# Three score banks and single vector steps in the head loop of a recurrence stage, with its maxima and constants moved into the first stage

## The reference

```python
q = layernorm(x); k = v = ctx
ig, fg = [q, k, v] @ Wi + bi, [q, k, v] @ Wf + bf            # (b, 16, 512)
log_D = tril(cumsum(log_sigmoid(fg)) differences) + ig       # (b, 16, 512, 512)
D = exp(log_D - max(log_D))
C = (qh @ kh.T / sqrt(32)) * D
h = (C / (max(|C.sum|, exp(-max)) + 1e-6)) @ vh
h = (h - mean) * rsqrt(var + 1e-6) * ln_scale                # over the 32 columns of a head
x = x + tanh(g) * h
```

## Time and profile before

| what | us |
| --- | --- |
| median of three runs | 1750.79 |
| profiled execution, its own time | 1748.16 |
| its span | 1746.40 |
| recurrence stage within it | 0 to 369.25 |
| first multiplication of a head (L645) starts | 94.29 |
| last head's product is added to OUT (L628) | 344.15 |
| PE, DVE, ACT, POOL busy in the span | 1389.4, 1243.4, 767.4, 321.9 |

### The profile page before, as it was taken

How to read it: one execution, slowest core, us unless ns; L and a number is a source line. 1 busy time by engine, 2 the same in 40 slices (tenths; PEclk the granted TensorE clock), 3 DMA queues, 4 the chain that set the end, 5 groups by cost and what they waited for, 6 DMA issues and landing times. The chain is left out here.

```text
span 1746.4 us, 24792 instructions
## 1 busy us (share of the span) xinstructions
PE 1389.4 (80%) x9060; PEld 788.7 (45%) x9060; DVE 1243.4 (71%) x1952; ACT 767.4 (44%) x1450; POOL 321.9 (18%) x233
## 2 busy tenths in 40 slices
PE   3589899735568798987487696877999999999997
PEld 2367677521233344433354464533444444444443
DVE  4354666676256777895799999858778877788764
ACT  2433444335334354432688797823333333333322
POOL 0021142244555455754000000000000000000000
PEclk9777888755789899999798798989999999999998
DMA  7012133214533324222503000000000000000000
GB/s 254 3 51 71 61 121 97 73 53 149 146 101 98 117 89 129 85 98 101 200 2 120 24 0 0 0 1 4 9 6 6 6 12 6 6 6 6 12 6 12
DMA packets 56494, 102.19 MB, mean 59 GB/s; under 512 B 9823, under 2 KB 20727, under 8 KB 56300
## 3 DMA queue, kind: packets, MB, share of 16 engines
q1 hardware_dynamic: 55148, 97.14, 17.1%
q0 software_dynamic: 1280, 4.20, 0.9%
HBM read 73.47 MB, written 27.66 MB: 58 GB/s over the span
## 5 line engine op out<-in xcount | busy, mean ns | idle before, releaser
L2047 PE MATMUL HG<-W1H,XT 128*128 128x512 f16 x512 | 166.7, 388 | 27.2 <-ACT XT L2008 20.7
L1521 PE MATMUL FD<-W0D,HH 128*128 128x512 f16 x512 | 159.2, 394 | 14.6 <-DMA W0D<-down_weights,IDX 11.0
L2047 PE MATMUL HU<-W1H,XT 128*128 128x512 f16 x512 | 163.2, 380 | 0.0
L2073 PE MATMUL HD<-W1H,HT 128*128 128x512 f16 x512 | 155.3, 380 | 0.0
L1515 PE MATMUL FG<-F,W0G 97*128 97x512 f16 x324 | 84.4, 394 | 49.8 <-DMA F<-features_kept 23.3
L318 ACT ACTIVATE DD<-E,TM 128x128 f32<-128x128 f32 x256 | 72.6, 370 | 115.8 <-PE E L411 115.6
L1768 ACT ACTIVATE PR<-A_S,NM,CM 128x512 f32<-128x512 f32 x128 | 99.5, 777 | 34.4 <-DVE NM L1909 34.4
L2016 ACT ACTIVATE SG<-HG,DS 128x512 f32<-128x512 f32 x64 | 43.9, 686 | 160.3 <-PE HU L2047 160.3
L2150 DVE SCALAR_TENSOR_TENSOR H<-HU,DS,SG 128x512 f32<-128x512 f32 x64 | 48.0, 750 | 87.4 <-ACT SG L2016 85.4
L1405 POOL TENSOR_TENSOR HL<-HM,HH 128x512 f16<-128x512 f32 x64 | 92.5, 1445 | 82.6 <-ACT HH L1444 82.0
L1521 PE MATMUL FD<-W0D,HL 128*128 128x512 f16 x256 | 100.8, 394 | 0.0
(11 more groups left out here) (333 smaller groups left out, 3376.7 us busy)
## 6 DMA issues: line engine op xcount, KB each, us to landing
VALP<-in_ffn_weights_dram SPq DMA_DIRECT2D x24, 512.0 KB, 3.5
VALQ<-in_ffn_weights_dram SPq DMA_DIRECT2D x24, 512.0 KB, 3.6
quantised_weights<-QQ SPq DMA_DIRECT2D x24, 512.0 KB, 2.8
X<-in_x_dram SPq DMA_DIRECT2D x8, 1024.0 KB, 6.2
CTX<-in_ctx_dram SPq DMA_DIRECT2D x8, 1024.0 KB, 5.5
W1H<-quantised_weights SPq DMA_DIRECT2D x3, 2048.0 KB, 10.5
W1L<-quantised_weights SPq DMA_DIRECT2D x3, 2048.0 KB, 15.2
F<-features_kept SPq DMA_DIRECT2D x16, 288.0 KB
```

Of the source, the lines that this page charges most:

```text
L1521: last = pe.matmul(DN[c][:, :], lhs[:, i, c * P:(c + 1) * P], W2[:, i, part, :], start=(i == 0 and n == 0), stop=(i == KI - 1 and n == 2))
L2047: ins = pe.matmul(bank[:, :], lhs, rhs, start=(i == 0), stop=(i == len(terms) - 1))
L2073: ins = pe.matmul(DN[0][:, :], HT[:, q, lp, k, :], W[:, 2, i * D:(i + 1) * D], start=(i == 0 and lp == 0 and W is WH), stop=(i == KI - 1 a ...
```

## The change

PSUM bank T[1] becomes a third score bank: head n uses QK[n % 3]; read_state writes T[0] too, and state(n) waits for take_read(n - 1). `scores` waits for one head less. DVE goes head by head, with one optional step behind each; where the steps stand is given by lists. Eleven of the 24 maxima stand in the first stage, and their loads on SP before the stores of the NP parts. The fillers behind weigh(2 pair) and behind scores are left out. The first scores and two decays stand ahead of the first state, and ACT takes the first state behind head 1. The block in front is gone: X of batch 0 is the first load, the constants are made between batch 0 and batch 1, WG and GLN are loaded behind batch 1's context, and ACT does the deviation of batch 1 before batch 0's copies, that of batch b + 1 before batch b's copies. MV and SD have a place for each batch.

```diff
+FINISH_HEADS = (2, 12)
+COEF_HEADS = (0, 1, 13, 14, 15)
+PEAKS_FIRST = 11
+PEAK_HEADS = {2: (0, 1, 4, 8, 13, 14, 15), 3: (1, 4, 8, 13, 14, 15)}
...
-    T = [ps("T0"), ps("T1")]
-    QK = [ps("QK0"), ps("QK1")]
+    T = [ps("T0")]
+    QK = [ps("QK0"), ps("QK1"), ps("QK2")]
...
             for b in range(B):
-                if b:
-                    sp.dma_start(X[:, b * NC:(b + 1) * NC, :], xr[b]).then_inc(x_in[b], 16)
+                sp.dma_start(X[:, b * NC:(b + 1) * NC, :], xr[b]).then_inc(x_in[b], 16)
+                if b == 0:
+                    sp.dma_start(CST[:, :], A["shape_constants"]).then_inc(consts_in, 16)
+                    for q, name in enumerate(("g_xattn", "g_ffn")):
...
                 sp.dma_start(ctx_room[b], ctx[b]).then_inc(ctx_in[b], 16)
-                if b == 0:
+                if b == 1:
...
             spline.load(sp)
+            peaks.transfers(sp, 0, PEAKS_FIRST)
...
                     sp.dma_start(CTX[:, :, :], ctx[b + 1]).then_inc(ctx_again, 16)
-                peaks.transfers(sp, b)
                 if b == 0:
+                    peaks.transfers(sp, PEAKS_FIRST, PEAKS_FIRST + 2)
+                elif b == 1:
                     spline.store(sp)
+                else:
+                    done = PEAKS_FIRST + 2 + sum(len(PEAK_HEADS[i]) for i in range(2, b))
+                    peaks.transfers(sp, done, min(Q_TILES, done + len(PEAK_HEADS[b])))
...
-            act.wait_ge(pre_dve, PRE_DVE)
+            act.wait_ge(eps_ready, 3)
+            deviation(0)
+            act.wait_ge(consts_in, 3 * 16)
+            nc.scalar.activation(tg[:, :], tg[:, :], ACT.Tanh).then_inc(tanh_ready, 1)
             act.wait_ge(pre_pool, 3)
+            deviation(1)
             for b in range(B):
-                deviation(b)
+                if b >= 1 and b + 1 < B:
+                    deviation(b + 1)
...
                 if pair:
-                    pe.wait_ge(c_ready, 2 * pair)
+                    pe.wait_ge(c_ready, 2 * pair - 1)
...
                 if n:
-                    pe.wait_ge(state_taken, n)
+                    pe.wait_ge(read_taken, n)
...
+            pe.wait_ge(tm_taken, 2)
+            scores(0)
+            decay(0)
+            decay(1)
+            pe.wait_ge(tm_taken, 5)
             state(0)
-            scores(0)
-            for n in range(4):
-                decay(n)
+            decay(2)
+            decay(3)
             for pair in range(HEADS // 2):
                 ahead = 2 * pair + 4
                 weigh(2 * pair)
-                fill(ahead)
                 decay(ahead)
                 if pair % 2 == 0:
                     read_state(pair // 2)
                     fill(ahead + 1)
                 if pair + 1 < HEADS // 2:
                     scores(pair + 1)
-                    fill(ahead + 1)
                 weigh(2 * pair + 1)
...
+            for n in range(PEAKS_FIRST - 2):
+                peaks.peak(v, n)
...
             own(v.tensor_scalar(MZ, ZF, 0.0, None, ALU.min))
             owned()
+            peaks.peak(v, PEAKS_FIRST - 2)
...
             v.tensor_tensor(RR, NM, PARTS3[:, 0:S], ALU.subtract).then_inc(r_ready, 1)
+            peaks.peak(v, PEAKS_FIRST - 1)
...
+            for n in range(HEADS):
+                b, h = divmod(n, NH)
...
+                if h % HG == 1:
+                    take_read(n // HG)
+                if n % 2 == 0 and n:
+                    take_pair(n // 2 - 1)
+                if b == 0 or (b == 1 and h in COEF_HEADS):
                     next(coefficients, None)
+                if b and FINISH_HEADS[0] <= h <= FINISH_HEADS[1]:
+                    if h == FINISH_HEADS[0]:
                         v.wait_ge(o_taken, b * PAIRS)
+                    next(last_batch, None)
+                if b >= 2 and h in PEAK_HEADS[b]:
+                    peaks.peak(v, peak)
+                    peak += 1
```

More of the change, by code:

```diff
@@ L320, in _ @@
                     ins.then_inc(d_ready, 1)
-                    if n % HG == HG - 1 and n > HG and n // HG < HEADS // HG:
+                    if n == 1:
+                        take_state(0)
+                    elif n % HG == HG - 1 and n > HG:
                         take_state(n // HG)
@@ L356, in gates @@
                 pe.wait_ge(t_taken, 16 * pair + 16)
+                if pair == 0:
+                    pe.wait_ge(pre_dve, PRE_DVE)
                 for k in range(2 * KD):
@@ L484, in pre, with constants, gate_weights @@
                 ins.then_inc(pre_dve, 1)
[L486 to L496, removed]
+            v.memset(EPS[:, 0:1], 1e-5).then_inc(eps_ready, 1)
+            v.memset(EPS[:, 1:2], 1.0).then_inc(eps_ready, 1)
+            v.memset(EPS[:, 2:3], 1e-6).then_inc(eps_ready, 1)
+            def constants():
+                pre(v.memset(ONE[:, :], 1.0))
+                v.wait_ge(consts_in, 3 * 16)
+                pre(v.tensor_copy(idb, idf))
+                pre(v.tensor_copy(idh, idf))
+                for c in range(NC):
+                    pre(v.tensor_copy(FUT[:, c, :], CST[:, P:2 * P]))
+                pre(v.tensor_copy(PICK[:, :], CST[:, 2 * P:2 * P + NH]))
+            def gate_weights():
+                v.wait_ge(w_loaded, 3 * 16)
+                pre(v.tensor_tensor(WG[:, 4:8, :], WG[:, 4:8, :], WG[:, 8:12, :], ALU.add))
+                v.wait_ge(tanh_ready, 1)
+                pre(v.tensor_scalar(GLN[:, :], GLN[:, :], tg[:, 0:1], -1.0, ALU.mult, ALU.mult))
+                assert n_pre[0] == PRE_DVE
             n_own = [0]
@@ L517, in _ @@
                 v.wait_ge(sd_ready, b + 1)
-                own(v.reciprocal(RS[:, :], SD[:, :]))
+                own(v.reciprocal(RS[:, :], SD[:, b, :]))
                 owned()
@@ L635, in _ @@
             coefficients = spline.vector_steps(v)
-            for pair in range(HEADS // 2):
-                b, pp = divmod(pair, PAIRS)
-                if pp == 0:
+            peak = PEAKS_FIRST
+            for n in range(HEADS):
+                b, h = divmod(n, NH)
+                if h == 0:
                     last_batch = finish(b - 1) if b else iter(())
-                v.wait_ge(qk_ready, pair + 1)
-                for n in (2 * pair, 2 * pair + 1):
-                    v.wait_ge(d_ready, n + 1)
-                    if n >= 2:
-                        v.wait_ge(pv_done, n - 1)
-                    v.scalar_tensor_tensor(out=CC[:, n % 2, :], in0=QK[n % 2][:, :], scalar=DH ** -0.5,
-                                           in1=DD[:, n % 4, :], op0=ALU.mult, op1=ALU.mult).then_inc(c_ready, 1)
-                if pp % 2 == 0:
-                    take_read(pair // 2)
-                if pair:
-                    take_pair(pair - 1)
-                if b == 0:
+                v.wait_ge(qk_ready, n // 2 + 1)
+                v.wait_ge(d_ready, n + 1)
+                if n >= 2:
+                    v.wait_ge(pv_done, n - 1)
+                v.scalar_tensor_tensor(out=CC[:, n % 2, :], in0=QK[n % 3][:, :], scalar=DH ** -0.5,
+                                       in1=DD[:, n % 4, :], op0=ALU.mult, op1=ALU.mult).then_inc(c_ready, 1)
+                if h % HG == 1:
[3 more added lines that the diff above has]
+                if b == 0 or (b == 1 and h in COEF_HEADS):
@@ L1156, in __init__, with transfers @@
         self.peak_ready, self.mx_ready, self.all_max = (nc.alloc_semaphore("p_" + n) for n in ("peak", "mx", "all_max"))
-    def transfers(self, sp, b):
-        for n in range(max(0, (b - 1) * PEAKS_B + 2), min(b * PEAKS_B + 2, Q_TILES)):
+    def transfers(self, sp, first, last):
+        for n in range(first, last):
             if n >= 2:
@@ L2281, in build_program @@
             used = []
-            mlstm_phase(nc, A, X, TG, CST, CST[:, 0:P], IDB[:, :], spline, peaks, used, stack)
+            mlstm_phase(nc, A, X, TG, CST, CST[:, 0:P], IDB[:, :], IDH[:, :], spline, peaks, used, stack)
         with ExitStack() as weights:
```

78 lines of the change are left out of this document (28 added, 50 removed).

## The result

The changed kernel takes 1675.26 us in the median of four runs (1671.69 to 1677.74), against 1752.04 for the kernel before in four: a ratio of 0.9545, with a 95% interval of 0.9497 to 0.9593. It is faster by some 77 us; 1666 was forecast, in a range of 1654 to 1706. One remark for later: where a kernel's ratio and its profiled execution seem to disagree (the kernel without fillers), the profiled execution was the longest of its runs and stands outside the ratio.

A forecast was written before the change was run, and what follows sets the result against it. TensorE was taken to bound the loop, through its work, idle time and work at 1.2 GHz. -72 - 9.3 + 0.5 - 1.6 - 2.3 = -84.7 from 1748.16 gave 1663.5, put at 1666 for the median; range 1654 to 1706.

The forecast's parts named there:

- The loop, forecast 178 us: Loop over 64 heads: 165.4 us of TensorE work plus 12.5 of gaps, all at 2.4 GHz, against 249.9: -72.
- The gaps behind head 11: Loop, head 11: the step waits for the scalar engine's square root, a gap of 1.2 us in three batches.
- The four of 1.4 us: Loop: with a maximum in head 4 or 8 of batches 2 and 3, CC(4k + 2) is 1.4 us late, four times.
- the 0.2 us in each group: Loop: CC(4k + 2) is 0.2 us late for its weigh, counted nine times in the gaps.
- under 2.1 us: Loop: all gaps stay below this length, so the forecast keeps 2.4 GHz throughout.
- Rival A: Loop: gaps of 1.2 to 1.4 us drop the clock, 7 x 5 = 35 us more: 1701; chance 0.23.
- rival D: Loop: without the two fillers the clock falls and doesn't come back, loop 334 us: 1822, slower; chance 0.03.
- The first stage, forecast -8.8: First stage: ZALL at 56.9 us instead of 66.20, -9.3, with +0.5 for the nine maxima.
- the earlier exponential: Behind the first scores and decays, before state(0): the first exponential starts 1.6 us earlier, -1.6.
- the bound: First stage: TensorE can be at 1.2 GHz in gates(0), which would double it; stage between -2 and -13.
- the nine maxima, +0.5: First stage, before t_ready: first tile lands at about 37.5, ninth reduced at 58.2, ZALL ready at 57.6: +0.5.
- The tail, forecast -2.3: Tail: L570 takes 0.27 us instead of 2.59, as POOL is through by then: -2.3.

The follow-up runs named there:

- pairs: Changed kernel with three score banks, but the vector engine's two products of a pair back to back and both optional steps behind them: 1748.6 us, ratio 0.997.
- second profile: The changed kernel run again, unchanged, to show scatter: 1674.7 us, ratio 0.9574, loop 177.5 us.
- thick: Changed kernel with all four fillers of a pair back, plus a useless 1.2 us vector operation behind head 11 of batches 1 to 3: 1684.8 us, ratio 0.9611.
- no fillers: Changed kernel with the fillers left in the loop and in state also left out: 1689.0 us, ratio 0.9589, loop 212.1 us.
- thin: Changed kernel plus a useless 1.2 us vector operation behind head 11 of batches 1 to 3: 1686.5 us, ratio 0.9649.
- two banks: Changed kernel with two score banks and two state banks, and scores waiting for both heads of the pair, as before the change: 1690.9 us, ratio 0.962.
- old, fewer fillers: Kernel before with the same two fillers of each pair left out, nothing else: 1758.8 us, ratio 1.0029.
- order only: Kernel before with the vector engine going head by head, one optional step behind each; two score banks, all fillers: 1719.1 us, ratio 0.9826.
- maxima in the loop: Changed kernel with 22 of the 24 maxima in the loop and two in the first stage: 1687.7 us, ratio 0.9634.
- early fillers: Changed kernel with the two fillers put back in the first two pairs only: 1672.2 us, ratio 0.9532.
- tuned: Changed kernel with early fillers, 8 maxima in the first stage and 16 in the loop, later deviations, and head 11 skipped in finishing batches 0 and 1: 1664.5 us, ratio 0.9484.

## Why the prediction was right, point by point

**The loop, forecast 178 us.** Measured 181.2 and 177.5. The reading that the vector order makes TensorE wait, and that the low clock behind these waits is the larger part of the cost, held: pairs brings both back. Three terms were off and nearly cancelled, which is luck. A group takes 10.80 us instead of 10.46, 5.4 us over sixteen; two of the four fillers that go had each covered 0.1 us of a weight load, and read_state takes 0.1 us more. The gaps are 4.6 to 5.8 us instead of 12.5. And the forecast had no 1.2 GHz at all, where one profile has 10 us of it at 96 us and the other 8 in the last heads. The gaps behind head 11 came as forecast (1.2 us; 0.90, 0.90 and 1.33). The four of 1.4 us behind the maxima of heads 4 and 8, and the 0.2 us in each group, did not come. The count had the product of head 4k ready just when its weigh starts. The vector engine is further ahead: in the second profile, batch 2, the product of head 4 ends at 187.83 and its weigh starts at 189.91, so that in spite of the maximum between them the product of head 6 (to 194.58) is still 0.3 us ahead of its weigh (194.92).

**Which gaps drop the clock.** The prediction kept 2.4 GHz because all gaps would be "under 2.1 us". The outcome was nearly right, the reason was not: 1.13 us drops it in pairs, 2.03 doesn't in the thick kernel, and without fillers it falls with no gap. Rival A, which put a chance on gaps of 1.2 us, has its mechanism in pairs, and in the changed kernel itself behind the last of the three gaps, where little work is left to be slowed; rival D has it in the kernel without fillers. (The prediction says that the clock stayed from 156 to 184 us without a gap; there is one of 0.57 us at 178.8, behind the state matmuls.)

**The first stage, forecast -8.8, and -1.6 for the earlier exponential.** Measured to the first product, -7.4 and -5.3 (94.3 before, 86.9 and 88.95 after) instead of -10.4. The steps up to ZALL came nearly to the microsecond: statistics at 6.35 (6.5), gates(0) at 32.20 (32.2), ZALL at 57.68 (56.9). The first half of gates(0) ran at 1.2 GHz (6.26 us against 3.63 in the earlier trace rows), as the bound had allowed. The term that was mis-sized is the nine maxima, +0.5: in nine profiles with this first stage ZALL to AZ takes 4.4 to 8.0 us, against 2.7 where they stand elsewhere, so they cost 1.7 to 5.3. The first tile was reduced at 39.84 instead of 37.5 (40.97 in the second profile); each further one took 2.4 us, as forecast (2.35), so that late start stayed to the end. Behind them L561, 0.48 us, now stands in the chain, which ran in idle time before. "The first exponential 1.6 us earlier" gave 0.6 in the first profile and nothing in the second (AZ to the first product: 25.4 before, 24.8 and 25.4 after).

**The tail, forecast -2.3.** Measured -1.5 and -1.9. In the first profile POOL's addition to X runs until 270.29 us, not far enough ahead, and the operation of the earlier trace rows takes 1.10 us instead of 2.59. In the second POOL is through at 267.27, 0.4 us before that operation, and it takes 0.26, as forecast. The mechanism is shown more sharply than the prediction had it: in all seven profiles in which POOL's addition is still running, the operation ends 0.12 to 0.14 us behind POOL's end, however long that is (0.94 to 2.59 us); in the other seven it takes 0.26. The row of the first profile:

```profile
269.32 1.10 DVE L606 SCALAR_TENSOR_TENSOR DN<-OUT 128x64 f32<-128x64 f32 x1
```

**The rest of the kernel.** Forecast no change. It was 1384.2 us against 1377.15, but in all other profiles, the two kernels with the old first stage among them, it lies between 1380.4 and 1384.7. The 1377.15 of the profile from which the sum was made is the lowest of all, some 4.5 us below the middle of the others; the forecast gave 2.6 of them back when it went from the profiled execution to the median, so some 2 of the 9 us between forecast and median are that. The other 7 (first profile) or 5 (second) are the recurrence stage: 3 to 5 us of the first stage, 0.4 to 0.8 of the tail, and in the first profile 3.3 of the loop, where the clock fell at 96 us.

## What to carry to other kernels

When two engines hand over in turns, cut the optional work of the engine that is waited for to one step per hand-over before anything else; a further buffer pays once that order stands (here 18 to 22 us with it, at most 5.5 without). Count a stall of TensorE at its length and at the half-speed work behind it: in the kernel before 27 us of gaps brought 87 us at 1.2 GHz, which cost some 43. A filler can be cheaper than its length, as it may cover the next weight load (7 us for 60 of them here, not 13), and without any the clock fell four times, so try fewer, not none. And maxima or other work moved into a "free" wait are bound by their own loads: give them a place where being late holds up nobody.

## What the runs showed of the hardware that was not expected

The granted clock does not go by the length of TensorE's last idle time alone. It fell with none over 0.3 us near it (no fillers, at 167 us; thin, at 203.7 us), some 2 us behind gaps of 0.36 to 0.62 us, for 3 to 4 us at a time (two banks, five places; two more are behind 1.05 and 1.32 us), and behind 1.13 us (pairs). Where the gap stood directly behind the state matmuls, it stayed through longer ones: 1.13 us (old, fewer fillers), 1.56 (order only), 2.02 twice (maxima in the loop), 2.03 twice (thick), 2.15 once of two times (thin). It fell behind 2.46 us (thick, maxima in the loop) and 2.58 us (thin) there too, and behind 1.33 us in three profiles of four (second profile of the changed kernel, early fillers, tuned; not the first profile). These last stand before head 12 of batch 3, behind which no decay and no filler is left to do. Ahead of the fall at 167 us without fillers TensorE had done, from 160.4 us on, a state, a read_state, scores, three weighs and two decays. Which of these things counts was not tested by itself. The same kernel, at the same place, fell in one execution and not in another.

The vector operation of the earlier trace rows, where it met POOL's addition, ended 0.12 to 0.14 us behind it, in seven profiles (0.94 to 2.59 us for an operation that takes 0.26 in the seven others).

The Trainium skill, "TensorE: Matmul & The Clock Gate", section "A second HAM failure mode: psum-queue depth-cycling", describes short idles between groups of matmuls as enough to make the clock swing. Two banks agrees, with gaps of 0.36 to 0.62 us; the kernel without fillers goes further, at 3.93 busy of 4.00 us.
